# Four reciprocal calls placed later in VectorE's tap order, in a fused conv-attention and mixture FFN block

## The reference, cut to what matters

```
qkv = conv2d(x, qkv_w)                                    # 1x1, 768 channels
agg = conv2d(conv2d(qkv, agg_dw_w, depthwise 5x5), agg_pw_w, grouped 1x1)
ms  = concatenate([qkv, agg])                             # two halves of heads, 8 channels a head
q, k = relu(q), relu(k);  v = concatenate([v, ones])
out = q @ (k^T v)
out = out[..., :-1] / (out[..., -1:] + 1e-15)             # the denominators
x   = x + batchnorm(conv2d(out, proj_w))
t   = t + sum_e weight_e * (gelu(LN(t) @ W1_e + b1_e) @ W2_e + b2_e)   # weights from the top 2 of a router
```

## Time and profile before

| | |
|---|---|
| median of 3 runs | 1735.21 us (1733.52 to 1737.08) |
| span of the profiled execution | 1727.4 us |
| TensorE matmul busy | 1398.5 us, 81% |
| VectorE busy | 1291.6 us, 75% |
| GpSimd busy | 1180.7 us, 68% |
| ScalarE busy | 931.2 us, 54% |
| the 32 reciprocals (L1027) | 30.4 us busy, 950 ns each |

### The profile page before, as it was taken

How to read it: one execution, slowest core, us unless ns; L and a number is a source line. 1 busy time by engine, 2 the same in 40 slices (tenths; PEclk the granted TensorE clock), 3 DMA queues, 4 the chain that set the end, 5 groups by cost and what they waited for, 6 DMA issues and landing times.

```text
span 1727.4 us, 20194 instructions
## 1 busy us (share of the span) xinstructions
PE 1398.5 (81%) x6652; PEld 793.5 (46%) x6652; DVE 1291.6 (75%) x1305; ACT 931.2 (54%) x1622; POOL 1180.7 (68%) x1017
## 2 busy tenths in 40 slices
PE   5414657569998899979997899879997899798998
PEld 2113455345463545445553645445544446454443
DVE  3999999999948997789958995799868896600100
ACT  3443434365646665655565564655666564544554
POOL 3573356347966797768875697768874677467776
PEclk7657777788999999989998899989998899898999
DMA  5100000000000100010001000010001000100000
GB/s 172 73 0 25 1 0 25 0 1 1 25 13 1 37 25 13 1 37 25 13 1 39 1 25 13 1 37 1 13 1 37 1 1 13 37 1 1 25 1 25
DMA packets 14270, 32.92 MB, mean 19 GB/s; under 512 B 2384, under 2 KB 5328, under 8 KB 13904
## 3 DMA queue, kind: packets, MB, share of 16 engines
q1 hardware_dynamic: 14160, 31.56, 5.2%
HBM read 23.17 MB, written 8.39 MB: 18 GB/s over the span
## 4 chain that ended last, share of the span: by engine, by line
PE 44%; DVE 19%; POOL 18%; issue 13%; ACT 4%; DMA 1%; POOLq 0%; ACTq 0%; SPq 0%; DVEq 0%
PE wbk L618 17%; DVE dacc L1139 17%; PE acc L631 13%; POOL dwo L933 6%; PE wbk L567 3%; POOL nrm L888 3%; PE wbk L593 3%; POOL gl L968 2%; POOL hb L965 2%; PE wbk L557 2%; PE wbk L582 1%; PE wbk L535 1%; POOL nrm L863 1%; POOL rb L861 1%; ACT dwo L683 1%
## 5 line engine op out<-in xcount | busy, mean ns | idle before, releaser
L1139 DVE SCALAR_TENSOR_TENSOR dacc<-qkvs,dww,dacc 128x930 f32<-128x930 f32 (+4 forms) x954 | 1052.9, 1187 | 0.5 <-issue 0.5
L968 POOL TENSOR_TENSOR gl<-hb,gh 128x512 f16<-128x512 f32 x256 | 302.1, 1180 | 21.4
L933 POOL TENSOR_TENSOR dwo<-dwo,tapb 128x992 f32<-128x992 f32 (+1 forms) x104 | 239.2, 2300 | 83.5 <-ACT tapb L688 74.7
L816 ACT ACTIVATE hb<-wbk,b1s 128x512 f32<-128x512 f32 x256 | 176.0, 687 | 210.1 <-PE wbk L618 209.9
L965 POOL TENSOR_SCALAR hb<-hb,ewg 128x512 f32<-128x512 f32 x256 | 184.8, 722 | 148.0 <-ACT gh L706 147.7
L631 PE MATMUL acc<-gh,w2h 128*128 128x512 f16 x512 | 199.0, 389 | 55.4 <-POOL gl L968 55.0
L631 PE MATMUL acc<-gh,w2l 128*128 128x512 f16 x512 | 198.5, 388 | 0.0
L631 PE MATMUL acc<-gl,w2h 128*128 128x512 f16 x512 | 198.5, 388 | 0.0
L706 ACT ACTIVATE gh<-hb,ewg 128x512 f16<-128x512 f32 x256 | 182.3, 713 | 0.0
L618 PE MATMUL wbk<-th,w1h 128*128 128x512 f16 x512 | 159.7, 395 | 4.9 <-ACT sum_b L802 2.4
L1027 DVE RECIPROCAL den<-den 128x128 f32<-128x128 f32 x32 | 30.4, 950 | 176.0 <-ACT den L791 176.0
(11 more groups left out here) (148 smaller groups left out, 2243.0 us busy)
## 6 DMA issues: line engine op xcount, KB each, us to landing
xa<-x SPq DMA_DIRECT2D x8, 1024.0 KB, 5.0
yr<-x SPq DMA_DIRECT2D x8, 1024.0 KB, 5.0
out<-yr SPq DMA_DIRECT2D x16, 512.0 KB, 2.8
dwo<-w SPq DMA_DIRECT2D x1, 2048.0 KB, 10.9
yr<-w SPq DMA_DIRECT2D x2, 1024.0 KB, 16.0
dwo<-w_qkv SPq DMA_DIRECT2D x1, 768.0 KB, 4.4
wp<-w_proj SPq DMA_DIRECT2D x1, 512.0 KB, 12.3
pw<-w_pw SPq DMA_DIRECT2D x16, 24.0 KB
```

What stands on the lines that cost most here:

```text
L816: last = nc.scalar.activation(hb[:, f % GB, :], b[:], ACT.Gelu, bias=b1s[:, f % FT:f % FT + 1], scale=1.0 / (X_SCALE * W_SCALE))
L933: ins = nc.gpsimd.tensor_tensor(d3[:, oy, ox], d3[:, oy, ox], t3[:, iy, ix], ALU.add)
L968: nc.gpsimd.tensor_tensor(gl[:, f % GB, :], hb[:, f % GB, :], gh[:, f % GB, :], ALU.subtract).then_inc(g_low, 1)
L1139: ins = nc.vector.scalar_tensor_tensor(out=dst[:, oy, ox], in0=i3[:, iy, ix], scalar=dww[:, m, tap:tap + 1], in1=a3[:, oy, ox], op0=ALU.mu ...
```

## The change

The four keys of `DIVIDE` move: half 1 from places 44 and 47 to 46 and 50, half 0 from places 104 and 107 to 116 and 127. The calls, their order among each other, their waits and what waits for them stay the same. In pair terms: the first call of half 1 goes from ahead of pair 0's copies to ahead of pair 1's first centre operation, the second from ahead of pair 1's second centre operation to two taps after it, and the calls of half 0 go from 12 and 15 operations into pair 2 to 24 and 35 operations into it. In the first image they go to the same numbers `n`, where pair 2 begins at 92 too.

```diff
--- before.py
+++ after.py
@@ -1080,7 +1080,7 @@
                 ew_task(j, par)
 
 
-            DIVIDE = {44: (2, 1, 0), 47: (2, 1, 1), 104: (1, 0, 0), 107: (1, 0, 1)}
+            DIVIDE = {46: (2, 1, 0), 50: (2, 1, 1), 116: (1, 0, 0), 127: (1, 0, 1)}
 
             CARRIED = {8: "max", 16: "route"}
             OWN = {128: "max", 136: "route"}
```

## The result

The changed kernel takes 1765.35 us (median of 4 runs, 1762.99 to 1768.53) against 1734.37 us, a ratio of 1.0178 (95% interval 1.016 to 1.0197). Measured a second time, beside other runs, it took 1764.6 us against 1729.56, ratio 1.0202 (1.0188 to 1.0215). It is slower by some 31 to 35 us. In the batch of the first four experiments one execution of the kernel before took 6624.96 us, and the ratios leave it out.

The account below looks back on a forecast made before the run. The prediction took VectorE to bound the first two filling steps, and GpSimd's base taps to set VectorE's start in full steps. Fill +42.3, full steps 0 and drain -6.0 gave +36.3 us, so 1771.5 us, range 1762 to 1781.

Parts of the forecast that it names:

- Step 1: First filling step: half 0's second reciprocal starts 22.0 us later, so image 1 starts 21.2 us later; bounds 19 and 25.
- Step 2: Second filling step: another 22.0 us at half 0, so the first full step starts 42.3 us late; bounds 38 and 50.
- rival (a): TensorE's clock stays low longer in the fill: +4 us in each of two steps, 1779.5 us; chance 0.07.
- Full steps: Five full steps: saved VectorE stalls become waits for GpSimd, 0 us, bounds -5 to +5; 4.5 us spare at half 0.
- signs of being wrong: Full-step scaling waits for the reciprocal, step distance changes by over 1 us, or first full step under 38 us late.
- Half 1: Calls moved 44 to 46 and 47 to 50: nothing shows in step 2, 0 us, bounds 0 and +1.
- The drain: Step 8: TensorE's 3.94 us wait for VectorE's last copies goes and its clock stays up: -6.0 us, bounds -3.9 and -6.6.
- The sum: Whole kernel: +42.3 + 0 - 6.0 = +36.3 us, new span 1763.7, time 1771.5 us.
- (b): Rival: slack in step 2 absorbs the second fill delay, +15 us, 1750 us; chance 0.04.
- (c): Rival: the fill's delay is hidden entirely and only the drain's gain is left, 1729 us; chance 0.04.
- (d): Rival: VectorE bounds the full steps, so each gives back 23 us, 1656 us; chance 0.03.
- (e): Rival: reciprocals come too late in full steps, beyond 4.5 us of lateness; at 8 us late +21, 1792 us; chance 0.03.

Follow-up runs that it names:

- the first four experiments: New places everywhere but the fill (0.9956), in the fill alone (1.024), in the full steps alone (1.0001), in step 8 alone (0.9966), each against the kernel before.
- The split by steps: New places only in some kinds of step, against the kernel before: fill alone 1.024, full steps alone 1.0001, step 8 alone 0.9966, all but the fill 0.9956.
- the filler in both kernels: 14 unread sums on VectorE at place 128 of each full step: in the changed kernel 1766.62 us (1.0215), in the kernel before 1783.72 us (1.0312).
- the call at 136: Kernel before with new places in the full steps alone, the last call at place 136 instead of 127: 1756.42 us, ratio 1.0169.

## Why the prediction was right, step by step

**What bounds the kernel.** Right: VectorE in the fill, the serial chain in the full steps. The split by steps, the filler in both kernels and the call at 136 each show it from another side. (The row that the prediction calls 948 is the one from 748 to 938 us.)

**Step 1, +21.2 us.** Counted from the first centre operation of pair 2 in step 1, which the executions reach a little apart (159.40 before, 158.32 after), VectorE's second centre operation of the next image came (227.40 - 158.32) - (207.79 - 159.40) = 20.7 us later. The pair of base additions took 4.74 instead of 5.53 us, as the step had it: this time VectorE stood idle beside it. No run moved half 0's two calls apart in the fill, so that the second one carries the delay rests on the chain shown above.

**Step 2, 42.3 us in all.** The maximum reached ScalarE 42.5 us later, 43.6 from the common point. The 1.3 us more than forecast are a sum: the scaling began 42.8 us late instead of 43.2, and the way from it to the end of the base additions took 34.7 instead of 33.1 us. That second part is rival (a) in small. In this execution TensorE waited 2.21 us for ScalarE at 378.44 and came back at the lower level (two 128x512 matmuls took 0.59 us before the wait and 1.06 us after it), so that its clock was 0.71 in the 8 us from 372 on and 0.90 in the 10 us behind them. The length of that wait alone doesn't decide it: the kernel before waited 3.22 us at the same place and kept the upper level. In the second profile of the changed kernel (that of its repeat) the clock was 0.92 and 1.00 there, as before the change (0.93 and 1.00), and the way took 33.0 us. Yet the maximum came 43.3 us late there too, since VectorE's two centre operations of pair 2 took 4.20 us beside GpSimd's work, where they take 2.49 in the other two. So the clock isn't the only thing that can add these 1 to 2 us.

These are the rows of the stretches (window, length, busy time of TensorE's matmuls and weight loads, VectorE, ScalarE and GpSimd, granted clock, DMA share and GB/s), first of the changed kernel, then of its second profile, then of the kernel before:

```profile
372.00:380.00 8.00, 5.79 (x17) 1.93 (x16) 5.98 (x8) 5.76 (x9) 6.70 (x4) 0.71 0.00 0
380.00:390.00 10.00, 9.66 (x35) 4.28 (x34) 0.00 (x0) 4.94 (x9) 0.00 (x0) 0.90 0.00 0
```

```profile
375.50:383.50 8.00, 4.85 (x20) 1.93 (x19) 5.94 (x8) 5.83 (x10) 6.66 (x4) 0.92 0.00 0
```

```profile
330.30:338.30 8.00, 4.78 (x20) 1.89 (x19) 8.00 (x9) 5.83 (x10) 6.68 (x4) 0.93 0.00 0
```

The second profile's centre operations:

```profile
329.12 4.20 DVE L1130 SCALAR_TENSOR_TENSOR dacc<-qkvs,dww,dwo 128x1024 f32<-128x1024 f32 x2
```

**Full steps, 0.** Right: 1.0001 (0.999 to 1.0011). One of my signs of being wrong was met to the letter, a change of the step distance by over 1 us. Between maxima the second full step took 192.6 us after and 188.1 before. But the five together changed by 1.4 us, from a mean of 190.7 to 191.0, and single steps scatter by more than 1 us within one kernel, so the sign was too tight. The estimate of 4.5 us to spare was measured as 4.6.

**Half 1, 0.** Right within 3 us, which is all that the time can show. In step 2 the estimate (0 to +1) left out that GpSimd's later work can fall beside VectorE's centre operations, 1.7 us in two of the profiles.

**The drain, -6.0 us.** Measured alone -5.9 by the ratio (-5.0 by the medians, the interval from -8.0 to -3.8). Both halves of the account are in the rows: TensorE's wait of 3.94 us is gone, and the clock stays up behind it.

**The sum.** +36.3 was put at 1771.5 us; the runs say +31.0 and +35.0, and 1765.35. The step that was off is the last one, the way from the span to the run's time. I took the 7.8 us between the span before (1727.4) and the median run (1735.21) as something that lies around the span. It isn't: in every execution on record the run's time is its span plus 1.7 to 1.8 us (1768.53 against 1766.8 in the profiled execution of the changed kernel), and the other 6 were the distance between a quick execution and a slow median. With 1.7 the sum would have given 1765.4, the measured time to a tenth. That would have been luck, since the quick execution from which it starts stood some 5 us below the median of 1734.37. The kernel before ran in 1734.37 us in the first measurement and in 1728.9 to 1730.5 in those of the experiments, while the changed kernel ran in 1765.35 and 1764.6: such a scatter of 5 us between measurements is as large as the miss.

**The rivals.** (b) and (c) fall with the fill changed alone (1.024). (d) falls with the full steps changed alone. (e) is a true mechanism with its threshold where it was put, and not reached by this change. (a) was put at 4 us in each of two steps; in step 1 the way from the scaling to the end of the base additions wasn't longer (28.6 against 29.9 us), and in step 2 it was longer by 1.7 us or not at all.

## What to carry to other kernels

A wait on an engine costs nothing as long as what starts that engine's next piece comes from elsewhere; look at what the engine waits for *after* the stall before counting the stall as a gain. A task that sits at a fixed place in one engine's in-order work has a different best place in each stage of a pipeline: in the fill the engine came to it late and each operation of delay was paid once in each of two steps, in the full steps the same move was free, with 4.6 us to spare. Where a table of places serves all stages, give each stage its own.

## What the hardware showed beside this

The full steps of one and the same kernel differ by 2.8 us with the same work, and the longer ones have the lower granted clock of TensorE. These are stretches between two maxima in the changed kernel (columns as above):

```profile
410.50:600.90 190.40, 169.69 (x824) 96.58 (x825) 159.01 (x163) 113.75 (x201) 145.50 (x124) 0.93 0.03 9
600.90:793.40 192.50, 173.23 (x832) 99.48 (x831) 159.02 (x162) 113.42 (x201) 146.35 (x125) 0.92 0.05 17
793.40:983.10 189.70, 167.64 (x823) 95.22 (x821) 159.17 (x162) 113.42 (x202) 145.31 (x125) 0.95 0.05 18
```

The step with clock 0.92 has 5.6 us more matmul time than the one with 0.95 and is 2.8 us longer; VectorE's busy time agrees to 0.2 us. That the clock is the cause isn't shown. The same goes for whole executions: the 17 of the kernel before that were measured beside the version with half 1 alone ran from 1724.31 us, at a mean granted clock of 0.898, to 1737.3 us, at 0.89. So 3 to 6 us between two profiles of the same kernel mean nothing, and a single profile pair (+39.4 us in span here) overstates what the runs show (+31 to +35).
